# A sixth product term for head 3, a product buffer and counts for each of two sums, weights prepared on GpSimd, and other orders in the five engine loops

## The chip, the cores and the metric

The kernel runs on one core of a Trainium2 chip. The metric is the device time of one execution in microseconds (us), the median of a few executions. Work is issued to five engines that run their own instruction streams: TensorE (PE; its weight loads are shown as PEld), VectorE (DVE), ScalarE (ACT), GpSimd (POOL) and SyncE (SP, which only issues transfers). They wait for one another through semaphores.

## The reference, cut to what matters

Two sequences of 4096 tokens with 512 features go through a layer norm and then through two branches whose results are added to the input. All arithmetic is float32, H = 4 heads of 128.

```python
xn = layernorm(x)
# branch 1: attention by the delta rule in chunks of 32, with a convolution path
q, k, v = (silu(causal_conv4(xn @ W)) for W in (Wq, Wk, Wv))
delta_out = delta_rule_chunkwise(q, k, v, sigmoid(xn @ Wb))   # state S, triangular inverses
outs = [dwconv_causal(v, w) for w in (ms_w3, ms_w15, ms_w31)] # 3, 15 and 31 taps
ms_out = (per_head(concat(outs)) @ kernel_mix_w) @ channel_mixer_w
wts = softmax(gelu([xn, mean|ms|, mean|delta|, mean|v|] @ w1 + b1) @ w2 + b2)
o = rmsnorm(wts[0]*ms_out + wts[1]*delta_out + wts[2]*v) * o_norm_w
out = x + o @ Wo
# branch 2: token-shift FFN on xn
out += sigmoid(xr @ W_r) * (relu(xk @ W_k)**2 @ W_v)
```

## The kernel before, in words

The tokens are cut into 32 steps of 128 tokens of both sequences. Every engine runs the loop `for i in range(NS + 2)`, and three steps are in flight: in pass `i` the front of step `i` (norm, projections `project`, `copy_raw`), the middle of step `i - 1` and the end of step `i - 2`. There are 31 passes (i = 2 to 32) that hold all of middle and end. The order of the calls in each engine's loop is written out by hand, call by call, and it is the order in which the engine executes: an engine whose next instruction waits does nothing else.

**The tap sums.** The 3-, 15- and 31-tap convolutions make 12 blocks of 128 channels, three a head, in `my[h % 2]`. ScalarE writes the first tap (`first_taps`, L1106), VectorE adds the others one by one (`taps`, L1531, one instruction of 128x256 a tap). For some leading taps ScalarE makes the products instead (`multiply_taps`, L1117, three activations into `prod`), and GpSimd issues a DMA that adds `prod` to `my` (`add_taps`, L457). `LEAD[h]` says how many taps of a head VectorE does not do: one for heads 0 and 1, two for head 2 (one product), five for head 3 (four products). So there are five adding DMAs a step and 196 - 27 = 169 taps for VectorE. All products share one buffer `prod` and one count, so a product waits for the addition before it.

**The inverse.** ScalarE scales the Gram matrices (`scale_B`, L983). SyncE writes them to HBM and reads 64 blocks of 16 rows back (`rows_out`, `Bu`). GpSimd inverts the blocks column by column (`invert_units`, L431 to L439). SyncE writes and reads again (L355, then L364, four transfers into `Yq`). TensorE then joins blocks: `inverse_W` (L570), `inverse_Z` (L581), `join_W` (L590), `join_Z` (L602, L604), `half_W` (L613), `half_X` (L621), with small steps of VectorE (`turn_Y`, `mask_W`, `step_Y`) and ScalarE (`copy_W`, `spread_X`, `join_X`, `copy_half_W`, `join_half_X`) between them. `key_state` (L630) and `solve` (L637) need the full inverse.

**Other names of the argument.** `channel_mix` (L699) ends the convolution path; `copy_ms` reads it. `turn_o` (L746) transposes the normalized output (`normalize_o`, L1214, which needs GpSimd's `invert_o`); `attend` (L754) multiplies by Wo. `ffn_key` (L662) needs `mix_in` (L1507) from VectorE, which needs `mix_half` (L1072) from ScalarE. `project` (L516) runs in six pairs 0 to 5; pair 4 needs pair 2 copied (`copy_raw(i, 2)`, L894). `prepare_weights` (L1384 to L1395) runs once, on VectorE at the start of pass 2.

## Time and profile before

| | |
|---|---|
| time, median of 3 runs | 3527.82 us (3523.88 to 3529.14) |
| the profiled execution: its own time | 3519.07 us |
| its span, first to last instruction | 3517.3 us |
| mean granted TensorE clock | 0.98 |
| TensorE busy | 94% of the span |
| VectorE busy | 90% |
| ScalarE busy | 78% |
| GpSimd busy | 23% |

All times in the rows are counted from the start of the span. The busy share of an engine is a sum over stages; a step has about 105.5 us, and what ends the waits inside one step is read from the timeline of one step.

### The profile page before, as it was taken

To read this page: it belongs to the slowest core of one execution; us is meant where nothing else is said; L and a number is where in the kernel's file an instruction comes from. 1 tells how busy PE (TensorE), PEld (TensorE's weight loads), DVE (VectorE), ACT (ScalarE), POOL (GpSimd) and SP (SyncE) were. 2 spreads that over 40 slices of the span, in tenths; PEclk is the share of its full clock that TensorE was granted. 3 is DMA by queue.
4 is the path that set the end of the run, shared out by engine and by line. 5 is a ranking of instruction groups with operands and counts; after the bars stand their busy time and mean duration, and the time that the engine had idled before them with its cause. 6 is when DMAs were issued, how large, how long until landed. Compare 5 with 4: busy or idle time off the path is not lost.

```text
span 3517.3 us, 69963 instructions
## 1 busy us (share of the span) xinstructions
PE 3315.3 (94%) x22848; PEld 2447.8 (70%) x22848; DVE 3165.9 (90%) x7856; ACT 2758.2 (78%) x9144; POOL 807.7 (23%) x1489
## 2 busy tenths in 40 slices
PE   6899999999999999999999999999999999999986
PEld 5677777667777667776677776777766677767754
DVE  6999998999999999989999999999899899989993
ACT  5677888778887778787778887778877788877774
POOL 2022221122221222221222211222212222112220
PEclk8999999999999999999999999999999999999998
DMA  6022221122211122211222111222111222112220
GB/s 183 11 50 51 50 40 33 29 51 51 50 32 33 37 51 51 50 28 25 49 51 51 36 38 29 50 51 50 32 33 38 51 50 43 35 24 51 45 44 7
DMA packets 188307, 154.92 MB, mean 44 GB/s; under 512 B 111804, under 2 KB 146108, under 8 KB 187688
## 3 DMA queue, kind: packets, MB, share of 16 engines
q0 software_dynamic: 31744, 79.70, 13.1%
q1 hardware_dynamic: 156200, 70.76, 7.7%
q8 instruction: 182, 2.98, 0.3%
q14 instruction: 181, 1.48, 0.1%
HBM read 51.34 MB, written 52.95 MB: 30 GB/s over the span
## 4 chain that ended last, share of the span: by engine, by line
PE 35%; DVE 25%; ACT 21%; issue 9%; DMA 7%; POOL 2%; ACTq 0%; DVEq 0%; POOLq 0%; SPq 0%
DVE my L1531 19%; PE dense L721 6%; DMA my<-prod 5%; PE dense L674 5%; PE dense L678 5%; PE dense L662 3%; ACT my L1106 3%; PE small L690 2%; ACT dense L1136 2%; PE cell L644 2%; PE cell L645 2%; PE cell L637 2%; ACT kT L926 1%; DMA rows_out<-Bm 1%; ACT xsh L856 1%
## 5 line engine op out<-in xcount | busy, mean ns | idle before, releaser
L1531 DVE SCALAR_TENSOR_TENSOR my<-vT,mw,my 128x256 f32<-128x256 f32 x5408 | 2245.4, 480 | 38.9 <-DMA my<-prod 24.3
L721 PE MATMUL dense<-xsh,w 128*128 128x256 f32 x2048 | 483.2, 382 | 3.9
L397 POOL TENSOR_SCALAR vare<-xsq 128x2 f32<-128x2 f32 x32 | 6.2, 194 | 2081.8 <-ACT xsh L856 2081.8
L721 PEld LDWEIGHTS dense<-xsh,w 128*128 128x128 f32 x2048 | 369.4, 190 | 72.3 <-ACT xr L1168 11.1
L1079 ACT ACTIVATE ka<-dense 128x512 f32<-128x512 f32 x64 | 38.2, 597 | 319.3 <-PE dense L662 319.3
L662 PE MATMUL dense<-xk,wfk 128*128 128x256 f32 x1024 | 250.1, 400 | 22.0 <-DVE xb L1591 16.8
L662 PEld LDWEIGHTS dense<-xk,wfk 128*128 128x128 f32 x1024 | 198.4, 199 | 74.9 <-issue 47.0
L674 PE MATMUL dense<-wr,xr 128*128 128x512 f32 x512 | 235.4, 603 | 0.0
L516 PE MATMUL front<-xsh,wq 128*128 128x256 f32 x1024 | 231.9, 379 | 0.0
L678 PE MATMUL dense<-wfv,ka 128*128 128x512 f32 x512 | 230.2, 592 | 0.0
L516 PE MATMUL front<-xsh,wv 128*128 128x256 f32 x1024 | 228.7, 381 | 0.8 <-ACT xsh L871 0.8
L516 PE MATMUL front<-xsh,wk 128*128 128x256 f32 x1024 | 227.9, 379 | 1.4 <-ACT raw L894 1.4
L1117 ACT ACTIVATE prod<-vT,mw 128x256 f32<-128x256 f32 x480 | 211.0, 513 | 22.5 <-DMA my<-prod 22.0
L754 PE MATMUL dense<-wo,ms 128*128 128x512 f32 x512 | 228.2, 598 | 0.0
L699 PE MATMUL dense<-cm,ym 128*128 128x512 f32 x512 | 225.0, 592 | 0.0
L516 PEld LDWEIGHTS front<-xsh,wq 128*128 128x128 f32 x1024 | 192.0, 190 | 38.9 <-issue 14.8
L516 PEld LDWEIGHTS front<-xsh,wk 128*128 128x128 f32 x1024 | 193.5, 189 | 30.6 <-ACT raw L894 3.3
L516 PEld LDWEIGHTS front<-xsh,wv 128*128 128x128 f32 x1024 | 193.0, 191 | 27.3 <-issue 1.1
L457 POOL DMA_DIRECT2D my<-prod x160 | 146.4, 915 | 235.0 <-ACT my L1106 197.9
L690 PE MATMUL small<-my,km 128*128 128x256 f32 x768 | 193.0, 388 | 0.1
L439 POOL TENSOR_TENSOR Xu<-Xu,Tu 64x28 f32<-64x28 f32 (+3 forms) x448 | 182.4, 407 | 35.1
L436 POOL TENSOR_TENSOR Tu<-Bu,Xu 64x28 f32<-64x28 f32 (+3 forms) x448 | 181.7, 406 | 30.2
(182 smaller groups left out, 6803.2 us busy)
## 6 DMA issues: line engine op xcount, KB each, us to landing
my<-prod POOLq DMA_DIRECT2D x160, 384.0 KB, 4.2
xa<-in_x SPq DMA_DIRECT2D x32, 512.0 KB, 4.2
rows_out<-Bm SPq DMA_DIRECT2D x64, 256.0 KB, 4.3
out<-xb POOLq DMA_DIRECT2D x32, 512.0 KB, 14.7
Yq<-units_out SPq DMA_DIRECT2D x128, 32.0 KB, 2.1
w<-in_w SPq DMA_DIRECT2D x1, 2048.0 KB, 17.2
Bu<-rows_out SPq DMA_DIRECT2D x32, 64.0 KB, 2.9
units_out<-Xu SPq DMA_DIRECT2D x32, 64.0 KB, 2.5
```

The source lines that it names most:

```text
L436: e.tensor_tensor(Tu[:, 0:n, 0:j + 1], Bu[:, j, j + 1:HQ][:, :, None].broadcast_to([UNITS, n, j + 1]), Xu[:, j, 0:j + 1][:, None, :].broad ...
L439: left = e.tensor_tensor(Xu[:, j + 1:HQ, 0:j + 1], Xu[:, j + 1:HQ, 0:j + 1], Tu[:, 0:n, 0:j + 1], ALU.subtract)
L516: i = e.matmul(by_batch(front[pair % 2][:, c * W:(c + 1) * W]), wt[:, k, hs(c0 + c)], xsh[s % 2][:, k, :, 1:1 + P], start=(k == 0), stop=( ...
L662: i = e.matmul(dense[pair][:, c * W:(c + 1) * W], wfk[:, k, hs(2 * pair + c)], xk[:, k, :], start=(k == 0), stop=(k == CB - 1))
L674: i = e.matmul(dense[0][:, :], xr[:, k, hs(b)], wr[:, k, :], start=(k == 0), stop=(k == CB - 1))
L678: i = e.matmul(dense[1][:, :], ka[:, k, hs(b)], wfv[:, k, :], start=(k == 0), stop=(k == CB - 1))
L690: i = e.matmul(s_mix, km[:, p, :], my[h % 2][:, p, :], start=(p == 0), stop=(p == 2))
L699: i = e.matmul(dense[b][:, :], ym[:, k, hs(b)], cm[:, k, :], start=(k == 0), stop=(k == CB - 1))
L721: e.matmul(by_batch(o), w1[:, k, hs(2 * pair + c)], xsh[s % 2][:, k, :, 1:1 + P], start=(k == 0), stop=False)
L754: i = e.matmul(dense[b][:, :], ms[:, b, hs(h)], wo[:, h, :], start=(h == 0), stop=(h == H - 1))
L1117: i = e.activation(by_batch(prod[:, p, :]), vT[s % 2][:, c, :, off:off + P], ACT.Copy, scale=mw[:, col:col + 1])
L1531: i = e.scalar_tensor_tensor(o, vT[s % 2][:, c, :, off:off + P], mw[:, col:col + 1], o, ALU.mult, ALU.add)
```

## The change

`LEAD[3]` goes from 5 to 6: ScalarE makes one more product for head 3 (three activations), GpSimd issues one more adding DMA, VectorE does three taps less, in each step. Heads 0 and 2 on the one side, 1 and 3 on the other get a product buffer and a pair of counts of their own (`prod[h % 2]`, `tap_products[h % 2]`, `taps_added[h % 2]`). `prepare_weights` moves from VectorE to GpSimd, at the start of pass 2, and is written with other instructions (13 in place of 15 on the engine). The calls in the loops of GpSimd, TensorE, ScalarE and VectorE stand in another order.

```diff
-LEAD = (1, 1, 2, 5)
-ADDED = [sum(LEAD[:h]) - h for h in range(H + 1)]
+LEAD = (1, 1, 2, 6)
+ADDED = [LEAD[h] + LEAD[h + 2] - 2 for h in range(2)]
...
-        prod = sb("prod", P, 3, W)
+        prod = [sb(f"prod{i}", P, 3, W) for i in range(2)]
...
+        def add_index(h, r):
+
+            return r if h < 2 else LEAD[h - 2] - 1 + r
+
         def adds_before(s, h, r):
 
-            return taps_added, 16 * (s * ADDED[H] + ADDED[h] + r)
+            return taps_added[h % 2], 16 * (s * ADDED[h % 2] + add_index(h, r))
...
+            def prepare_weights():
...
+                e.wait_ge(split_in, 16 * (2 + PARTS * PARTS))
+                whole, taken = (t[0:NROW, :, :].rearrange("p b d -> p (b d)") for t in (ms, dl))
+                for k in range(CB):
+                    then(e.tensor_scalar(wo[:, k, :], wo[:, k, :], onw[:, 0:1], None, ALU.mult))
+                then(e.tensor_copy(ident16[:, :], ident))
+                then(e.tensor_copy(w1x[:, :], whole))
+                for j in range(1, PARTS):
+                    later = cst[0:NROW, C_PART + j:C_PART + j + 1]
+                    then(e.tensor_scalar(taken, w1x[:, :], later, None, ALU.mult))
+                    then(e.tensor_tensor(whole, whole, taken, ALU.subtract))
+                    then(e.tensor_copy(w1x[:, :], whole))
...
             def add_taps(s, h, r):
                 e.wait_ge(*tap_zero.upto(s, h))
-                e.wait_ge(*tap_products.upto(s, ADDED[h] + r))
-                e.dma_start(my[h % 2][:, :, :], prod[:, :, :], accum_op=ALU.add).then_inc(taps_added, 16)
+                e.wait_ge(*tap_products[h % 2].upto(s, add_index(h, r)))
+                e.dma_start(my[h % 2][:, :, :], prod[h % 2][:, :, :], accum_op=ALU.add).then_inc(taps_added[h % 2], 16)
...
+                if i == 2:
+                    prepare_weights()
...
             def multiply_taps(s, h, r):
 
-                if s or ADDED[h] or r:
+                if s or add_index(h, r):
                     e.wait_ge(*adds_before(s, h, r))
...
                 if c:
                     turn_o(i - 2, 0)
-                if f:
-                    project(i, 4)
-                if c:
                     turn_o(i - 2, 1)
                     attend(i - 2, 0)
                     attend(i - 2, 1)
```

**TensorE, from the last projections to the join.** Before, in the stretch from `project(i, 3)` on: `front<-xsh,wk` are the projections of pairs 2 and 3, `front<-xsh,wq` is `project(i, 4)`, `turn<-cst,vT` is `turn_tokens(i - 1, 3)`.

```order
L516 MATMUL front<-xsh,wk 128x256 x16
L746 MATMUL dense<-cst,dl 128x128 x4
L516 MATMUL front<-xsh,wq 128x256 x8
L746 MATMUL dense<-cst,dl 128x128 x4
L754 MATMUL dense<-wo,ms 128x512 x8
L662 MATMUL dense<-xk,wfk 128x256 x8
L570 MATMUL cell<-Yq,Bm 32x16 x32
L581 MATMUL cell<-Wq,Xq 32x16 x32
L662 MATMUL dense<-xk,wfk 128x256 x8
L590 MATMUL cell<-Yq,Bm 32x32 x16
L545 MATMUL turn<-cst,vT 128x128 x4
```

After (the same stretch; line numbers are those of the changed file, L786 is `attend`, L694 `ffn_key`, L602 and L613 `inverse_W` and `inverse_Z`, L622 `join_W`):

```order
L548 MATMUL front<-xsh,wk 128x256 x16
L662 MATMUL cell<-S,kT 128x128 x4
L778 MATMUL dense<-cst,dl 128x128 x8
L786 MATMUL dense<-wo,ms 128x512 x8
L577 MATMUL turn<-cst,vT 128x128 x4
L694 MATMUL dense<-xk,wfk 128x256 x8
L577 MATMUL turn<-cst,vT 128x128 x4
L602 MATMUL cell<-Yq,Bm 32x16 x32
L613 MATMUL cell<-Wq,Xq 32x16 x32
L622 MATMUL cell<-Yq,Bm 32x32 x16
```

`project(i, 4)` no longer stands between the two `turn_o`, `key_state(i - 1, 1)` stands ahead of them, both `turn_tokens` of v stand around the first `ffn_key`, and the second `ffn_key` no longer stands between `inverse_Z` and `join_W`.

**TensorE, from the join to the solve.** Before, from the last instruction of `join_Z`:

```order
L604 MATMUL cell<-Wq,Xq 32x32
L674 MATMUL dense<-wr,xr 128x512 x4
L678 MATMUL dense<-wfv,ka 128x512 x4
L613 MATMUL cell<-YW,Bm 64x64 x8
L621 MATMUL cell<-X,YW 64x64 x8
L630 MATMUL cell<-S,kT 128x128 x4
L637 MATMUL cell<-y,X 128x128 x8
```

After (L645 is `half_W`, L653 `half_X`, L706 and L710 `ffn_out(i - 1, 0)`, L662 `key_state(i - 1, 0)`):

```order
L636 MATMUL cell<-Wq,Xq 32x32
L694 MATMUL dense<-xk,wfk 128x256 x8
L645 MATMUL cell<-YW,Bm 64x64 x8
L548 MATMUL front<-xsh,wq 128x256 x8
L653 MATMUL cell<-X,YW 64x64 x8
L706 MATMUL dense<-wr,xr 128x512 x4
L710 MATMUL dense<-wfv,ka 128x512 x4
L662 MATMUL cell<-S,kT 128x128 x4
L669 MATMUL cell<-y,X 128x128 x8
```

The second `ffn_key` and `project(i, 4)` (L548) stand around `half_W` now, and `ffn_out` behind `half_X`.

**GpSimd, the second half of the inversion.** Before, from the eighth column's last subtraction (L457 is the adding DMA, `add_taps`):

```order
L439 TENSOR_TENSOR Xu<-Xu,Tu 64x6x10
L436 TENSOR_TENSOR Tu<-Bu,Xu 64x5x11
L439 TENSOR_TENSOR Xu<-Xu,Tu 64x5x11
L436 TENSOR_TENSOR Tu<-Bu,Xu 64x4x12
L439 TENSOR_TENSOR Xu<-Xu,Tu 64x4x12
L436 TENSOR_TENSOR Tu<-Bu,Xu 64x3x13
L439 TENSOR_TENSOR Xu<-Xu,Tu 64x3x13
L436 TENSOR_TENSOR Tu<-Bu,Xu 64x2x14
L439 TENSOR_TENSOR Xu<-Xu,Tu 64x2x14
L436 TENSOR_TENSOR Tu<-Bu,Xu 64x15
L439 TENSOR_TENSOR Xu<-Xu,Tu 64x15
L457 DMA my<-prod 128x768
```

After (L484 is the adding DMA):

```order
L463 TENSOR_TENSOR Tu<-Bu,Xu 64x5x11
L466 TENSOR_TENSOR Xu<-Xu,Tu 64x5x11
L484 DMA my<-prod 128x768
L463 TENSOR_TENSOR Tu<-Bu,Xu 64x4x12
L466 TENSOR_TENSOR Xu<-Xu,Tu 64x4x12
L463 TENSOR_TENSOR Tu<-Bu,Xu 64x3x13
L466 TENSOR_TENSOR Xu<-Xu,Tu 64x3x13
L463 TENSOR_TENSOR Tu<-Bu,Xu 64x2x14
L466 TENSOR_TENSOR Xu<-Xu,Tu 64x2x14
L463 TENSOR_TENSOR Tu<-Bu,Xu 64x15
L466 TENSOR_TENSOR Xu<-Xu,Tu 64x15
L484 DMA my<-prod 128x768
```

An adding DMA, that of head 3's fourth product, now stands inside the inversion; the fifth stands behind it, where the fourth stood.

## Rows read from the trace of the kernel before

**Rows 1.** Windows: stretch, its length, PE, PEld, DVE, ACT, POOL busy, granted clock.

```profile
1004.09:1109.57 105.48, 102.05 (x716) 75.34 (x715) 98.46 (x245) 86.10 (x286) 25.22 (x46) 1.00 0.21 42
1084.90:1109.57 24.67, 24.67 (x107) 16.08 (x106) 22.70 (x57) 20.62 (x76) 0.00 (x0) 1.00 0.00 1
```

**Rows 2.** Timeline of one step, VectorE: start, length, line, [idle before <-releaser].

```profile
1004.09 0.18 DVE L1541 TENSOR_TENSOR frest<-ft,fparts 128x24 f32<-128x24 f32 x1 [1.94 <-ACT fparts L1145]
...
1068.27 11.92 DVE L1531 SCALAR_TENSOR_TENSOR my<-vT,mw,my 128x256 f32<-128x256 f32 x30
```

**Rows 3.** Timeline of the same step, TensorE.

```profile
1048.00 0.66 PE L746 MATMUL dense<-cst,dl 128*128 128x128 f32 x4 [0.41 <-ACT dl L1214]
1048.49 3.63 PE L516 MATMUL front<-xsh,wq 128*128 128x256 f32 x16
1051.95 0.60 PE L746 MATMUL dense<-cst,dl 128*128 128x128 f32 x4
...
1059.98 3.69 PE L662 MATMUL dense<-xk,wfk 128*128 128x256 f32 x16 [0.55 <-DVE xb L1591]
1063.60 0.73 PE L570 MATMUL cell<-Yq,Bm 32*32 32x16 f32 x64
1064.82 0.72 PE L581 MATMUL cell<-Wq,Xq 32*32 32x16 f32 x64 [0.50 <-DVE Wq L1476]
1065.47 3.72 PE L662 MATMUL dense<-xk,wfk 128*128 128x256 f32 x16
1069.12 0.69 PE L590 MATMUL cell<-Yq,Bm 32*32 32x32 f32 x32
...
1079.90 1.14 PE L621 MATMUL cell<-X,YW 64*64 64x64 f32 x16 [0.68 <-ACT YW L1027]
1081.71 1.16 PE L630 MATMUL cell<-S,kT 128*128 128x128 f32 x8 [0.67 <-ACT X L1032]
```

**Rows 4.** Timeline of the same step, ScalarE.

```profile
1014.84 1.30 ACT L1117 ACTIVATE prod<-vT,mw 128x256 f32<-128x256 f32 x3
...
1021.32 0.84 ACT L1168 ACTIVATE xk<-dense,b 128x256 f32<-128x256 f32 x2 [0.97 <-PE dense L724]
...
1027.75 2.15 ACT L983 ACTIVATE Bm<-cell,g 128x128 f32<-128x128 f32 x8
...
1049.45 1.26 ACT L1214 ACTIVATE dl<-dl,rro 128x128 f32<-128x128 f32 x4
```

**Rows 5.** Timeline of the same step, GpSimd: the inversion's first and last, one adding DMA.

```profile
1037.29 0.44 POOL L431 TENSOR_SCALAR Xu<-Bu 64x15 f32<-64x15 f32 x1 [0.70 <-DMA Bu<-rows_out]
...
1050.23 0.93 POOL L457 DMA_DIRECT2D my<-prod  x1
...
1055.82 0.32 POOL L439 TENSOR_TENSOR Xu<-Xu,Tu 64x15 f32<-64x15 f32 x1
```

**Rows 6.** DMA view, stretch 1004 to 1110: issues, KB each, median us to landing.

```profile
my<-prod POOLq DMA_DIRECT2D x5, 384.0 KB, 4.3
...
Yq<-units_out SPq DMA_DIRECT2D x4, 32.0 KB, 2.2
```

**Rows 7.** Timeline of the same step, SyncE's queue.

```profile
1058.69 2.26 SPq L364 DMA_DIRECT2D Yq<-units_out  x4
```

**Rows 8.** Timeline at pass 2, VectorE (first and last of 15) and TensorE.

```profile
93.86 2.05 DVE L1384 TENSOR_SCALAR wo<-wo,onw 128x512 f32<-128x512 f32 x4
...
105.59 0.69 DVE L1395 CAST w1x<-dl 108x1024 bf16<-108x1024 f32 x1
...
106.66 1.06 PE L590 MATMUL cell<-Yq,Bm 32*32 32x32 f32 x32 [8.99 <-DVE Yq L1481]
```

**Rows 9.** Lines by form: two GpSimd instructions of different size, mean ns.

```profile
L439 POOL TENSOR_TENSOR Xu<-Xu,Tu 64x60 f32<-64x60 f32 x64 | 32.7, 511 | 5.0
L439 POOL TENSOR_TENSOR Xu<-Xu,Tu 64x15 f32<-64x15 f32 x32 | 10.3, 323 | 2.5
```

**Rows 10.** Windows, columns as in Rows 1: a stretch at the first join.

```profile
1489.40:1492.80 3.40, 3.40 (x10) 2.68 (x9) 3.36 (x10) 0.99 (x8) 0.00 (x0) 0.50 0.34 84
```

More of the change, by code:

```diff
@@ L777, in tensor_program @@
                 if c:
+                    hidden(i - 2, 1)
                     hidden(i - 2, 2)
@@ L820, in tensor_program @@
                 if k:
+                    turn_tokens(i - 1, 2)
                     ffn_key(i - 1, 0)
+                    turn_tokens(i - 1, 3)
                     inverse_W(i - 1)
                     inverse_Z(i - 1)
+                    join_W(i - 1)
+                    join_Z(i - 1)
                     ffn_key(i - 1, 1)
-                    join_W(i - 1)
-                    turn_tokens(i - 1, 3)
-                    join_Z(i - 1)
+                    half_W(i - 1)
+                if f:
+                    project(i, 4)
+                if k:
+                    half_X(i - 1)
                     ffn_out(i - 1, 0)
-                    half_W(i - 1)
-                    half_X(i - 1)
                     key_state(i - 1, 0)
@@ L1345, in scalar_program @@
                 if c:
+                    square_o(i - 2, 1)
+                    normalize_o(i - 2, 0)
                     normalize_o(i - 2, 1)
@@ new lines, in vector_program @@
+                    taps(i - 2, 3, 12, 14)
+                    taps(i - 2, 3, 15, 17)
+                    taps(i - 2, 3, 18, 20)
+                    taps(i - 2, 2, 36, 37)
+                    taps(i - 2, 3, 8, 9)
+                    taps(i - 2, 3, 21, 22)
+                    taps(i - 2, 2, 52, 53)
+                    taps(i - 2, 3, 22, 23)
+                    taps(i - 2, 3, 24, 25)
+                    taps(i - 2, 3, 11, 12)
+                    taps(i - 2, 3, 27, 28)
+                    taps(i - 2, 3, 14, 15)
@@ new lines, in vector_program @@
+                    taps(i - 2, 3, 25, 26)
+                    taps(i - 2, 3, 17, 18)
+                    taps(i - 2, 3, 28, 29)
+                    taps(i - 2, 3, 20, 21)
+                    taps(i - 2, 3, 30, 31)
+                    taps(i - 2, 2, 37, 38)
+                    taps(i - 2, 3, 31, 32)
+                    taps(i - 2, 3, 33, 34)
+                    taps(i - 2, 3, 23, 24)
+                    taps(i - 2, 3, 36, 37)
+                    taps(i - 2, 2, 53, 54)
+                    taps(i - 2, 3, 34, 35)
@@ L1691, in vector_program @@
                     taps(i - 1, 0, 0, 1)
+                    taps(i - 1, 1, 7, 8)
+                    taps(i - 1, 1, 6, 7)
                 if c:
@@ L1797, in vector_program @@
                 if k:
-                    taps(i - 1, 2, 36, 37)
-                    taps(i - 1, 2, 51, 52)
+                    mix_in(i - 1)
+                    taps(i - 1, 2, 47, 49)
                 if c:
@@ L1802, in vector_program @@
                 if k:
[L1803 to L1806 removed]
+                    taps(i - 1, 2, 30, 31)
+                    taps(i - 1, 2, 49, 50)
+                    taps(i - 1, 2, 34, 35)
+                    taps(i - 1, 2, 50, 52)
+                    taps(i - 1, 3, 1, 2)
+                    taps(i - 1, 3, 0, 1)
                     turn_Y(i - 1, 0)
                     mask_W(i - 1)
[L1809 to L1810 removed]
+                    taps(i - 1, 3, 4, 5)
+                    step_Y(i - 1)
+                    taps(i - 1, 3, 3, 4)
+                    turn_Y(i - 1, 1)
+                    taps(i - 1, 3, 7, 8)
         N_ZEROED = 13
[L1813 removed]
+        N_SCALED = CB + 2 + 3 * (PARTS - 1)
         plans = [tap_plan(h) for h in range(H)]
```

403 lines of the change are left out of this document (169 added, 234 removed).

## The prediction

> **What bounds the kernel now.** I read the table first: TensorE is busy for 94% of the span, VectorE for 90%. Such shares don't say which engine ends a step, so I took one step out of the middle, from one `frest` of VectorE, at 1004.09 [rows 2], to the next. It is 105.48 us long, and in it TensorE is busy 102.05 us, VectorE 98.46, ScalarE 86.10, GpSimd 25.22 [rows 1]. TensorE stands still for 3.4 us a step, all others for more. The last 24.67 us of the step have no gap on TensorE at all [rows 1].
>
> The second view is TensorE's timeline of that step [rows 3]. The reader is to look at the brackets: 0.41 us before `turn_o`, 0.55 before `ffn_key`, 0.50 between `inverse_W` and `inverse_Z`, 0.68 before `half_X`, 0.67 before `key_state`. From `inverse_W` at 1063.60 to the step's end only 1.85 us are gaps. So whatever is put into TensorE's queue behind `inverse_W` lengthens the step by its own length, except for what it fills of those 1.85 us.
>
> The third view says what `inverse_W` itself waits for. ScalarE ends `scale_B` at 1029.90 (1027.75 + 2.15) [rows 4]; the blocks go through HBM; GpSimd starts on them at 1037.29 and ends at 1056.14 (1055.82 + 0.32) [rows 5]; SyncE issues the four reads of `Yq` until 1060.95 (1058.69 + 2.26) [rows 7]; 2.2 us later they have landed [rows 6], at 1063.15. TensorE takes them at 1063.60. That leaves 0.45 us of slack. So a step has two parts in series: from the end of `channel_mix` over ScalarE, HBM, GpSimd and HBM to `Yq` (not shortened by an idle TensorE), and from `inverse_W` to the end of `channel_mix` (TensorE alone). The step is their sum.
>
> **The change, part by part.**
>
> *Three taps less on VectorE.* Thirty taps take 11.92 us [rows 2], 0.395 each from start to start, so 1.19 us a step go. VectorE is not on either part of the sum except in `turn_Y`, `mask_W` and `step_Y`; the relief is hidden under TensorE's work. Counted at 0; at most -1.19.
>
> *The sixth product.* Three activations take 1.30 us of ScalarE [rows 4], the issue of the DMA 0.93 us of GpSimd [rows 5], and it lands 4.3 us later [rows 6]. What counts is where it stands. Ahead of `scale_B`, the new order of ScalarE has one product and `first_taps(0)` more (2 x 1.3 us) and one `short_first` and some halo copies less (about 1.1 us, by my estimate from the 1.30 of three such activations); the wait of 0.97 us before `gelu_hidden` [rows 4], which was for TensorE, is filled by it. About 0.4 us more come from `copy_ms(1)` standing right behind `copy_ms(0)`. 2.6 - 1.1 - 0.97 - 0.4 is 0.1: `scale_B` ends where it did (-0.5 to +0.5). In GpSimd's stretch from `Bu` to the last column, three adding DMAs stand where two stood: +0.93. `Yq` lands at 1064.1, 0.45 us later than TensorE took it before. **+0.45** (0 to +1).
>
> *TensorE up to `inverse_W`.* `project(i, 4)` is gone from between the two `turn_o`. It took 3.46 us (1048.49 to 1051.95) [rows 3] there while ScalarE ended `normalize_o(1)`, at 1050.71 [rows 4]. Its new place in ScalarE's order brings it no earlier: `square_o(1)` waits behind a product that needs the previous addition, and GpSimd has an adding DMA between the two `invert_o`. I put its end at 1050.4. TensorE arrives at `turn_o(1)` at about 1048.2 and stands for 2.2 us. `attend` begins at 1051.0, `mix_in` still ends near 1059 since `mix_half` is behind the same work of ScalarE, `ffn_key(0)` ends at 1062.9, `turn_tokens` at 1063.3, and `Yq` is not there before 1064.1. Nothing is won in this part.
>
> *TensorE from `inverse_W` on.* Added: `project(i, 4)`, +3.46. Gone: `turn_tokens(3)`, four transposes like those of `turn_o`, 0.66 [rows 3]. Filled: the gaps of 0.68 and 0.67 in the half step, -1.35. The second `ffn_key` (3.65 us, 1065.47 to 1069.12 [rows 3]) no longer covers the hand-over from `inverse_Z` to `join_W`; `turn_tokens` no longer covers that to `join_Z`. The only such hand-over that is uncovered now, `mask_W`, costs 0.50 [rows 3]; the two others go the same way (one or two small VectorE instructions between two groups of small products), so 2 x 0.50 = +1.0 (+0.5 to +1.6). Together 3.46 - 0.66 - 1.35 + 1.0 = **+2.45**.
>
> A step becomes 2.9 us longer (range 1.5 to 3.9), 108.4 us. 31 passes: **+90 us** (47 to 121).
>
> *Weights on GpSimd.* On VectorE they took from 93.86 to 106.28, and TensorE stood for 8.99 us because `step_Y` was behind them [rows 8]. That stall goes: **-9**. GpSimd has 13 instructions over 9344 elements of a partition and can begin where VectorE did, near 93. `copy_o` of step 0 needs the result first. The join would now be near 98 (106.66 - 8.99), and behind it stand 10.8 us up to `half_X` and 1.8 more up to `key_state` in the old order (1069.12, 1079.90, 1081.71), with the 3.65 of `ffn_key` and the 3.46 of `project(i, 4)` added in the new one [rows 3]: about 118, and some 3 us of solve and outputs. No row has GpSimd at this size. Below, it needs the 12.4 us of VectorE; above, its slope between 15 and 60 elements, (511 - 323)/45 = 4.2 ns an element [rows 9], gives 39 us, which would end at 132 and cost some 11 us. I take it as hidden, because the slope comes from instructions that read through a stepped pattern, and plain rows should be nearer the low end. The Trainium skill, GPSIMD Engine Reference, section 3.1, has a two-input add of 2048 floats at 4497 ns on GpSimd and 2293 on VectorE; by that ratio the weights take about 25 us, end near 118, and stay hidden.
>
> The sum: own time 3519.07 + 90 - 9 = 3600. The runs' median stands 8.75 us above the profiled execution, so 3609.
>
> **The rivals.**
>
> *The relief reaches the end (faster).* For it: all of TensorE's 3.4 us a step are waits for others, VectorE is nearly as loaded as TensorE, and the half step's 1.35 us are filled in any case. It decides for it if `normalize_o(1)` ends 2 us earlier than I put it, so that no gap opens at `turn_o` and TensorE gets through its first part early, and if `Yq` is there by 1062, through an earlier `scale_B`. Then a step loses about 1.1 us: 3519 - 34 - 9 + 9 = 3485. Against it: the inversion's 18.85 us on GpSimd [rows 5] and four passages of HBM are the same. Chance 0.18.
>
> *Gains and losses cancel (no change).* `project(i, 4)` brings 3.46 us but lies where TensorE would stand anyway, because VectorE's taps for `kernel_mix` end the step. Against it: 24.67 us without a gap at the end [rows 1]. It needs +0.3 us a step: 3528. Chance 0.07.
>
> *The clock falls at the joins.* In a step further on, the granted clock was 0.50, its lower level (1.2 GHz), just after `inverse_W` [rows 10], and the `ffn_key` that stands there took 5.41 us in place of the 3.72 of [rows 3]. What came before were small products and a wait. In the new order four such groups with three waits follow one another, without `ffn_key`. If the clock falls once in most steps, that is +1.7 us each, 25 to 50 us: 3635 to 3660. In the half step the cause goes away, which pays part of it back. The Trainium skill, TensorE: Matmul & The Clock Gate, part 1, says that the array falls to half its clock when it has not been busy, which is the direction that the row shows. Chance 0.2, as a part of the slower case.
>
> *The five additions of head 3 come late.* Five rounds of 1.3 + 0.9 + 4.3 us [rows 4 to 6] are 32.5 us. The first product can be ready ahead of `first_taps(3)`, which stands behind `scale_B` and `normalize`, near 1031.6 in my count; so the fifth addition lands at 1063 to 1064. VectorE then stands for `taps(3)` in front of `turn_Y` for up to 1 us, at the very place where `Yq` arrives. It would add 0 to 31 us and is in the range.
>
> **How the numbers follow.** Slower by the sum above, with or without the clock: 0.75; faster 0.18; within 0.2% (7 us, about what a measurement of this kernel can tell) 0.07. The likeliest case's own range is 3560 (1.5 us a step) to 3660 (3.5 us a step and the clock). For eight times in ten I reach down to 3505.
>
> **What would show it.** Right: a step near 108.4 us; TensorE idle about 2 us before `turn_o`; gaps before `inverse_W`, `inverse_Z`, `join_W` and `join_Z`, together 2 to 3 us; none before `half_X` and `key_state`; VectorE idle more than the 7 us of a step now; no stall of 9 us at pass 2. Wrong: a step under 105 us, which would mean that `scale_B` ends earlier and moves `Yq` with it, or that TensorE's queue has less work behind `inverse_W` than I count.

## The result, and the profile after

The changed kernel takes 3692.39 us (median of 4 runs, 3689.91 to 3694.21), the kernel before 3525.9 in the runs beside it. The ratio is 1.0471, with a 95% interval from 1.0455 to 1.0486: slower by 166 us. I had forecast 3609 and a range up to 3660. The direction was right; the loss is twice what I worked out. Where a kernel had an execution in a slower state, at a lower clock, that one is left out of its median.

The profiled execution took 3689.91 us, with a span of 3688.1 and a mean granted clock of 0.955. The first view is the windows of the changed kernel, with the columns of [rows 1]: the prologue up to the first `frest`, the 31 steps, what is left, one step, and a stretch behind the joins of a later step.

```profile
0.00:153.60 153.60, 111.76 (x696) 86.83 (x697) 110.86 (x254) 85.79 (x266) 46.19 (x73) 0.88 0.41 113
153.60:3637.60 3484.00, 3247.69 (x22036) 2401.01 (x22034) 3026.80 (x7476) 2697.25 (x8909) 789.48 (x1455) 0.96 0.22 43
3637.60:3688.10 50.50, 27.69 (x118) 18.27 (x118) 6.86 (x16) 20.32 (x65) 3.63 (x5) 0.80 0.08 11
374.69:483.86 109.17, 103.59 (x716) 77.00 (x715) 98.10 (x242) 87.45 (x289) 25.20 (x47) 0.98 0.22 45
1111.00:1117.80 6.80, 5.01 (x68) 4.21 (x68) 6.80 (x19) 4.88 (x15) 0.00 (x0) 0.50 0.35 86
```

The kernel before has this row for its own 31 steps:

```profile
150.20:3465.50 3315.30, 3175.56 (x22036) 2344.31 (x22034) 3044.75 (x7570) 2653.12 (x8817) 778.88 (x1424) 0.99 0.21 41
```

Of the 170.8 us between the spans, the prologue holds +3.4, the steps +168.7, the rest -1.3. A step has 112.39 us on the mean (3484.00 / 31) against 106.94. TensorE is given the same 22036 matmuls and is busy 72 us longer with them, at a mean clock of 0.96 instead of 0.99. I added up the stretches at 0.50 in the record of the granted clock, by their place in a step, over the first 30 of the 31 steps (the last one has another 23.9 us before and 27.3 us after):

| kernel | behind `inverse_W` | near `turn_o` | half step | all |
|---|---|---|---|---|
| before | 6, 23.9 us | none | 10, 37.5 us | 61.4 us |
| changed | 29, 194.6 us | 13, 54.6 us | none | 249.2 us |

If TensorE had work in all of them, they cost half their length: 94 us of the 168.7 are the clock, 75 us (2.4 a step) are the rest. That is an estimate. A second way gives nearly the same: the 72 us of longer busy time, and 27 us more in which TensorE stands and waits for nothing that the profile shows. The changed kernel has 21 such places in its steps, the kernel before 7, and 17 of the 21 begin within 2 us of a fall of the clock. That this time goes with the clock is argued from the places alone. One ends at 1112.22, in the middle of the 32 products of `join_W`; it begins 0.1 us before a fall:

```profile
1112.22 0.53 PE L622 MATMUL cell<-Yq,Bm 32*32 32x32 f32 x12 [1.38 <-issue]
```

The second view is TensorE's timeline of the step at 374.69, one of the two shortest, with a single stretch of 3.4 us at 0.50; it answers to [rows 3].

```profile
418.67 0.60 PE L778 MATMUL dense<-cst,dl 128*128 128x128 f32 x4
420.87 0.66 PE L778 MATMUL dense<-cst,dl 128*128 128x128 f32 x4 [1.60 <-ACT dl L1243]
421.36 7.11 PE L786 MATMUL dense<-wo,ms 128*128 128x512 f32 x16
...
429.51 3.72 PE L694 MATMUL dense<-xk,wfk 128*128 128x256 f32 x16 [0.60 <-DVE xk L1511]
433.07 0.60 PE L577 MATMUL turn<-cst,vT 128*128 128x128 f32 x4
433.90 0.72 PE L602 MATMUL cell<-Yq,Bm 32*32 32x16 f32 x64 [0.23 <-DMA Yq<-units_out]
435.11 0.72 PE L613 MATMUL cell<-Wq,Xq 32*32 32x16 f32 x64 [0.50 <-DVE Wq L1480]
436.23 0.69 PE L622 MATMUL cell<-Yq,Bm 32*32 32x32 f32 x32 [0.40 <-DVE Yq L1485]
...
438.43 5.41 PE L694 MATMUL dense<-xk,wfk 128*128 128x256 f32 x16
443.77 1.14 PE L645 MATMUL cell<-YW,Bm 64*64 64x64 f32 x16
444.84 3.73 PE L548 MATMUL front<-xsh,wq 128*128 128x256 f32 x16
448.50 1.14 PE L653 MATMUL cell<-X,YW 64*64 64x64 f32 x16
```

Nearly each row is one that the prediction named. TensorE stands 1.60 us for `turn_o(1)`. `Yq` is the last to arrive at `inverse_W` (0.23). The four groups of small products follow with bare hand-overs. `project(4)` fills what was the gap in front of `half_X`. What I had only as a rival is the row at 438.43: the second `ffn_key` takes 5.41 us in place of 3.72. In most steps it is worse (5.94 on the mean of 29 steps; means over 29 steps leave out the first two of the 31).

### The profile page after: what moved, and what is told of

Same layout as the page of the kernel before. It is cut to its first block and busy times, and to the rows that moved or that the text cites. A ratio compares the mean times of both kernels' runs of the same rounds, so it can differ in the third digit from the quotient of the medians.

```text
span 3688.1 us, 70018 instructions
## 1 busy us (share of the span) xinstructions
PE 3387.1 (92%) x22848; PEld 2506.1 (68%) x22848; DVE 3144.5 (85%) x7745; ACT 2803.4 (76%) x9240; POOL 839.3 (23%) x1533
## 5 line engine op out<-in xcount | busy, mean ns | idle before, releaser
L694 PE MATMUL dense<-xk,wfk 128*128 128x256 f32 x1024 | 305.8, 463 | 23.2 <-DVE xk L1511 19.9
L1146 ACT ACTIVATE prod<-vT,mw 128x256 f32<-128x256 f32 x576 | 252.2, 506 | 81.2 <-DMA my<-prod 81.1
L694 PEld LDWEIGHTS dense<-xk,wfk 128*128 128x128 f32 x1024 | 236.4, 237 | 76.2 <-DVE xk L1511 19.1
L484 POOL DMA_DIRECT2D my<-prod x192 | 173.7, 905 | 373.8 <-ACT my L1135 291.4
L786 PE MATMUL dense<-wo,ms 128*128 128x512 f32 x512 | 250.5, 646 | 0.0
L548 PE MATMUL front<-xsh,wv 128*128 128x256 f32 x1024 | 231.9, 384 | 8.7 <-ACT xsh L900 8.6
L548 PE MATMUL front<-xsh,wq 128*128 128x256 f32 x1024 | 235.1, 382 | 0.0
L706 PE MATMUL dense<-wr,xr 128*128 128x512 f32 x512 | 233.6, 599 | 0.0
L548 PE MATMUL front<-xsh,wk 128*128 128x256 f32 x1024 | 230.4, 381 | 3.1 <-ACT raw L923 2.7
L710 PE MATMUL dense<-wfv,ka 128*128 128x512 f32 x512 | 230.2, 592 | 0.0
L548 PEld LDWEIGHTS front<-xsh,wv 128*128 128x128 f32 x1024 | 192.9, 191 | 41.2 <-ACT xsh L900 13.8
L548 PEld LDWEIGHTS front<-xsh,wq 128*128 128x128 f32 x1024 | 191.8, 190 | 40.9 <-issue 14.8
L548 PEld LDWEIGHTS front<-xsh,wk 128*128 128x128 f32 x1024 | 191.7, 190 | 36.6 <-ACT raw L923 10.8
L786 PEld LDWEIGHTS dense<-wo,ms 128*128 128x128 f32 x512 | 104.5, 210 | 123.5 <-issue 122.4
L1071 ACT ACTIVATE Bm<-cell,g 128x128 f32<-128x128 f32 x256 | 70.2, 369 | 154.0 <-PE cell L669 154.0
```

What stands on the lines that cost most here:

```text
L484: e.dma_start(my[h % 2][:, :, :], prod[h % 2][:, :, :], accum_op=ALU.add).then_inc(taps_added[h % 2], 16)
L548: i = e.matmul(by_batch(front[pair % 2][:, c * W:(c + 1) * W]), wt[:, k, hs(c0 + c)], xsh[s % 2][:, k, :, 1:1 + P], start=(k == 0), stop=( ...
L694: i = e.matmul(dense[pair][:, c * W:(c + 1) * W], wfk[:, k, hs(2 * pair + c)], xk[:, k, :], start=(k == 0), stop=(k == CB - 1))
L706: i = e.matmul(dense[0][:, :], xr[:, k, hs(b)], wr[:, k, :], start=(k == 0), stop=(k == CB - 1))
L710: i = e.matmul(dense[1][:, :], ka[:, k, hs(b)], wfv[:, k, :], start=(k == 0), stop=(k == CB - 1))
L786: i = e.matmul(dense[b][:, :], ms[:, b, hs(h)], wo[:, h, :], start=(h == 0), stop=(h == H - 1))
```

## The experiments

Seventeen kernels ran. "Changed" is the changed kernel; medians are compared with the runs of the kernel before beside them (3522 to 3529 us).

### The joins and the clock

**Bare joins alone.** The kernel before, with one piece of TensorE's new order. On ScalarE the two calls that take the result of `ffn_key(1)`, `relu_key(1)` and `square_key(1)`, move back with it, behind `copy_tokens(3)`:

```diff
                     inverse_Z(i - 1)
-                    ffn_key(i - 1, 1)
                     join_W(i - 1)
                     turn_tokens(i - 1, 3)
                     join_Z(i - 1)
+                    ffn_key(i - 1, 1)
```

> The kernel before with one part of the new order: ffn_key(1) behind join_Z instead of between inverse_Z and join_W (on ScalarE relu_key(1) and square_key(1) follow it, behind copy_tokens(3)); project(4), VectorE and GpSimd as before. The hand-over from inverse_Z to join_W is bare, +0.4 us a step, 12 us in all. Theory A (clock at the joins): in most steps a stretch at half clock is added there, which costs 1.7 to 3.4 us each beyond what the kernel before loses already, 3575 to 3635. Theory C (the clock is a by-product of lateness elsewhere in the changed kernel): 3530 to 3545.

Measured: 3632.25 us, ratio 1.0317 (1.0296 to 1.0337). TensorE's timeline of one of its steps:

```profile
1097.33 0.73 PE L570 MATMUL cell<-Yq,Bm 32*32 32x16 f32 x64
1098.55 0.72 PE L581 MATMUL cell<-Wq,Xq 32*32 32x16 f32 x64 [0.49 <-DVE Wq L1476]
1099.66 0.34 PE L590 MATMUL cell<-Yq,Bm 32*32 32x32 f32 x9 [0.40 <-DVE Yq L1481]
...
1103.22 5.62 PE L662 MATMUL dense<-xk,wfk 128*128 128x256 f32 x16
```

The stretches at 0.50 behind `inverse_W` go from 6 with 23.9 us to 30 with 211.6 us, the changed kernel's picture with nothing else of the change in it than the two calls on ScalarE. Over all steps 167 us more are at 0.50; half of them is 84 us, of the 108 by which the steps grew (again an estimate: TensorE is busy 62 us longer, and stands 16 us more for nothing that the profile shows). The rest are bare waits: 0.40 us a step in front of `join_W`, and 0.4 us in front of `turn_tokens(3)` for ScalarE. This is what the clock rival said, at about twice its price.

**Is it the idle time?** If waiting lets the clock fall, then something to do in the waits should hold it. Three products that nobody reads, first of 128 x 128, then of 128 x 256:

```diff
                     inverse_W(i - 1)
+                    busy(i - 1)
                     inverse_Z(i - 1)
+                    busy(i - 1)
                     join_W(i - 1)
+                    busy(i - 1)
                     turn_tokens(i - 1, 3)
```

> The kernel before with the bare joins (3632 us measured) and one extra product of 128 x 128 that nobody reads in each of the three waits of the joins. If idle time lets the clock fall, most of the 84 us of clock come back, 3550 to 3590; if small products alone are enough for it to fall, 3625 to 3645.

> The kernel before with the bare joins and one extra product of 128 x 256 in each of the same three waits as the run with 128 x 128. By itself the longer product costs up to 0.2 us a place beyond the wait, some 15 us. If full-size work in the joins holds the clock: 3570 to 3605. If it is only time that is added: 3635 to 3650.

Measured: 3623.7 us (the middle of 3618.08 to 3639.93) and 3618.84 us (3601.72 to 3624.14), against 3632.25 without; the gain of the small filler is not clear of the noise. The small filler leaves 208 us at 0.50 of the 229 in the first 30 steps, the long one 137, but that one adds its own length: 0.70 us a piece in the timeline, where the hand-overs have 0.4 to 0.6. So idle time alone isn't the cause; with hardly an idle stretch left between `inverse_W` and `join_W`, the clock still falls. The long filler holds it in part, and costs nearly what the clock gives back. The same filler in the changed kernel:

> The changed kernel with three extra products that nobody reads, one 128 x 256 product of 0.38 us ahead of inverse_Z, of join_W and of join_Z, each inside a hand-over of 0.40 to 0.58 us; no order is changed and no work is taken away. Theory A in the form that idle time in the joins lets the clock fall: the dips go, 3590 to 3620 us, and the hand-overs stay as long. If it is the small products that count as little work, whatever stands in the hand-overs: 3685 to 3705.

Measured: 3661.87 us (3640.89 to 3670.4), 249 us at 0.50 become 147. Half of that is 51 us; 31 are left over after what the fillers cost.

### Putting pieces of TensorE's order back into the changed kernel

**`ffn_key(1)` back between `inverse_Z` and `join_W`.**

```diff
-                    join_W(i - 1)
-                    join_Z(i - 1)
                     ffn_key(i - 1, 1)
+                    join_W(i - 1)
+                    join_Z(i - 1)
                     half_W(i - 1)
```

> The changed kernel with one call moved on TensorE: ffn_key(1) stands again between inverse_Z and join_W. Theory A, the clock at the joins: a full group of large products in the middle of the joins keeps the granted clock up; the hand-over of 0.40 us and the 2.2 us that ffn_key(1) loses at half clock go, together some 3 us a step, 3600 us (3585 to 3625). Theory B, the clock falls for another reason (the wait at turn_o, the small products themselves): only the hand-over comes back, 3670 to 3685. Theory C, the time is in what is late for TensorE, above all Yq: no change, 3692.

Measured: 3780.03 us, ratio 1.0722 (1.0688 to 1.0756): 88 us slower than changed, outside every theory of mine. TensorE's timeline shows the cause at once:

```profile
1146.77 0.22 PE L634 MATMUL cell<-Xq,Wq 32*32 32x32 f32 x2 [0.57 <-ACT Wq L1039]
1151.07 1.96 PE L645 MATMUL cell<-YW,Bm 64*64 64x64 f32 x16 [3.60 <-ACT YW L1050]
```

In the new order `ffn_key(1)` covers the 3.5 us that ScalarE needs between `join_Z` and `half_W` (`spread_X`, `join_X`), which in the kernel before the first `ffn_out` covered. Taken away, it leaves a wait of 3.60 us, after which `half_W` and part of `project(4)` run at half clock (1.91 us in place of 1.14 and 5.66 in place of 3.64, on the mean of 29 steps). I had looked at what the move lays bare, but not at what the changed kernel had put the piece there for.

**Both covers.** `project(4)` between `join_Z` and `half_W`, `ffn_key(1)` in the joins; on ScalarE `copy_raw(2)`, which takes a part of the projections, goes ahead of `copy_W`:

```diff
+                    ffn_key(i - 1, 1)
                     join_W(i - 1)
                     join_Z(i - 1)
-                    ffn_key(i - 1, 1)
-                    half_W(i - 1)
                 if f:
                     project(i, 4)
                 if k:
+                    half_W(i - 1)
                     half_X(i - 1)
```

> The changed kernel with ffn_key(1) between inverse_Z and join_W and project(4) between join_Z and half_W (copy_raw(2) on ScalarE moved ahead of copy_W, so that it isn't behind join_X). The 3.5 us from join_Z to half_W, which the run with ffn_key(1) alone laid bare, is covered by project(4); the gaps before half_X comes back (0.68). Against the changed kernel: -0.4 for a hand-over, +0.68, and under theory A about -2 us a step of clock: 3640 (3620 to 3665). If the clock falls for what comes before the inverse (the wait at turn_o): 3690 to 3710.

Measured: 3715.47 us. Now `half_X` waits, 2.09 us on the mean instead of the 0.68 of [rows 3], because in the new order ScalarE has `relu_key(0)` and `square_key(0)` ahead of `copy_half_W`. The stretches at 0.50 become 205 us, so by half their length 22 us of clock came back, and the wait took more.

**`project(4)` back between the two `turn_o`.** On ScalarE `copy_raw(2)` goes back ahead of `normalize_o`, too:

```diff
                     turn_o(i - 2, 0)
+                if f:
+                    project(i, 4)
+                if c:
                     turn_o(i - 2, 1)
...
                     half_W(i - 1)
-                if f:
-                    project(i, 4)
-                if k:
                     half_X(i - 1)
```

> The changed kernel with project(4) back between the two turn_o, and copy_raw(2) with its halo back ahead of normalize_o on ScalarE; the joins stay bare. My sum's term for project(4) was +3.46 behind inverse_W against 1.35 of filled gaps: without it a step loses 2.1 us, 3627 us. Theory A adds that the dips of the clock near the two turn_o go (about 12 of 31 steps, some 2 us each), 3600 to 3630. Theory C, Yq ends the first part of the step and project(4) would lengthen that part as much as it shortens the second: 3680 to 3700.

Measured: 3653.77 us (3633.33 to 3662.77), 38 us less than changed. All but two of the stretches near `turn_o` go, and the wait in front of `inverse_Z` grows: the new order leaves the fifth addition of head 3 late in 2 of 29 steps, by 9.35 and 9.65 us, and VectorE stands for it in front of `turn_Y`. That is my fourth rival; the changed kernel itself shows it only as short waits of VectorE, 0.1 to 1.5 us in 13 of its 31 steps, at the place where `Yq` arrives. The hand-over behind them stays at 0.50 us in every step, so they cost next to nothing. Then both moves together:

> Both moves of the two runs before it together: ffn_key(1) between inverse_Z and join_W, project(4) between the two turn_o. If the effects add and TensorE's order explains the loss, 3530 to 3550 us, within 1% of the kernel before. If VectorE's, ScalarE's and GpSimd's new orders hold a large part of it, over 3590.

Measured: 3771.56 us (3749.14 to 3793.55), ratio 1.0702 (1.0636 to 1.0767). The pieces don't add: the 3.5 us in front of `half_W` are bare here too, and 365 us of the steps are at 0.50.

`project(4)` back and the fillers of 128 x 256 in the joins, without the second move:

> The changed kernel with project(4) back between the two turn_o and the three extra products in the hand-overs of the joins: the two measured alone gave -38 and -30 us. If the bare joins cost clock by themselves, the effects add or more: 3600 to 3625. If both act on one cause, 3640 to 3655.

Measured: 3689.4 us, 36 more than with `project(4)` back alone. The late fifth addition comes in 5 steps, and `half_X` waits 1.24 us on the mean: TensorE reaches it sooner than ScalarE.

### The term for `project(4)`

The kernel before with one call moved:

```diff
                     turn_o(i - 2, 0)
-                if f:
-                    project(i, 4)
-                if c:
                     turn_o(i - 2, 1)
...
                     half_W(i - 1)
+                if f:
+                    project(i, 4)
+                if k:
                     half_X(i - 1)
```

> The kernel before with project(4) alone moved, from between the two turn_o to between half_W and half_X; nothing else on any engine. My sum: nothing won ahead of inverse_W because ScalarE and GpSimd set the end of turn_o(1) and Yq's arrival, and +3.46 - 0.68 = 2.8 us a step behind it, 3522 + 86 = 3608 (3590 to 3640 with some clock lost at turn_o). If TensorE gets through its first part earlier by what it no longer does there: 3522 to 3550.

Measured: 3595.43 us, ratio 1.0199 (1.0169 to 1.023). The timeline of a step near its middle:

```profile
1184.15 0.66 PE L746 MATMUL dense<-cst,dl 128*128 128x128 f32 x4 [1.95 <-ACT dl L1214]
1184.64 8.81 PE L754 MATMUL dense<-wo,ms 128*128 128x512 f32 x16
...
1212.39 3.73 PE L516 MATMUL front<-xsh,wq 128*128 128x256 f32 x16
1216.05 1.14 PE L621 MATMUL cell<-X,YW 64*64 64x64 f32 x16
```

The shortest step goes from 105.41 to 108.15 us: +2.74, where the sum says 3.46 - 0.68 = 2.78. What `project(4)` took at `turn_o` is waited out as predicted: in that step TensorE stands 2.20 us for `turn_o(1)` and 0.7 us more than before in front of the first `ffn_key`, and `inverse_W` begins where it did. In 22 steps the clock falls at `turn_o` (`attend` 8.81 instead of 7.03), though in the first 30 steps it no longer falls in the half step. This move alone costs 69 us and the bare joins alone 110; their sum, 179, is near the 166 of the whole change, which proves little, since the pieces didn't add when they were put back.

### VectorE and the sixth product

**The sixth product taken out of the changed kernel.**

```diff
-LEAD = (1, 1, 2, 6)
+LEAD = (1, 1, 2, 5)
...
-                    add_taps(i - 1, 3, 4)
...
-                    multiply_taps(i - 1, 3, 4)
...
-                    taps(i - 2, 3, 72, 75)
+                    taps(i - 2, 3, 72, 78)
```

> The changed kernel with the sixth product alone taken out (LEAD 5, four additions for head 3, the three taps back on VectorE at the end of its list); all orders else as changed. It prices the sixth product inside the new orders: my term was +0.45 us a step, so 3678 (3660 to 3690). If the product chain in front of normalize_o and turn_o is what TensorE waits for at 47 us of the step, as in the run with the sixth product in the old orders (4.9 us of wait there), 3600 to 3660. If VectorE needed the relief: 3700 to 3730.

Measured: 3712.87 us, ratio 1.0532 (1.0508 to 1.0555), 20 us more than changed. TensorE's timeline has one row in each step that the changed kernel hasn't:

```profile
1157.39 1.56 PE L721 MATMUL small<-my,km 128*128 128x256 f32 x6 [0.99 <-DVE my L1533]
```

The last `kernel_mix` waits for VectorE's taps. So in the new orders the sixth product, with the three taps that it takes off VectorE, is worth 20 us; I had counted the taps at nothing.

**The sixth product put into the kernel before**, two product buffers with it, products (3, 1) to (3, 4) one place earlier, their additions earlier on GpSimd, and VectorE's taps in an order that fits them:

```diff
-LEAD = (1, 1, 2, 5)
+LEAD = (1, 1, 2, 6)
...
                     copy_raw(i, 1)
+                if k:
+                    multiply_taps(i - 1, 3, 2)
                 if c:
                     square_o(i - 2, 0)
...
                     normalize_o(i - 2, 0)
                 if k:
-                    multiply_taps(i - 1, 3, 2)
+                    multiply_taps(i - 1, 3, 3)
```

> The kernel before with the sixth product alone: LEAD 6 for head 3, two product buffers and counts, three taps a step less on VectorE, the order of TensorE untouched; products and additions one place earlier on ScalarE and GpSimd to make room. My sum has +0.45 us a step for it (Yq later by one issue of 0.93 us on GpSimd), 3540 (3526 to 3556). If VectorE's relief reaches the end: 3500 to 3515. If the fifth addition is late for the taps in front of turn_Y: 3540 to 3580.

Measured: 3724.83 us, ratio 1.058 (1.0556 to 1.0605). ScalarE's and TensorE's timelines:

```profile
1103.39 1.31 ACT L1125 ACTIVATE prod<-vT,mw 128x256 f32<-128x256 f32 x3 [1.65 <-DMA my<-prod]
...
1107.66 1.28 ACT L1222 ACTIVATE dl<-dl,rro 128x128 f32<-128x128 f32 x4
1111.56 1.31 ACT L1125 ACTIVATE prod<-vT,mw 128x256 f32<-128x256 f32 x3 [2.62 <-DMA my<-prod]
```

```profile
1108.99 1.12 PE L754 MATMUL dense<-cst,dl 128*128 128x128 f32 x4 [3.46 <-ACT dl L1222]
```

Each product waits in ScalarE's queue for the addition before it, and `square_o` and `normalize_o` wait behind it. TensorE stands 4.88 us on the mean in front of `turn_o(0)` (3.48 in the middle one of the steps). How much of this is the product and how much my placing of it, this run doesn't separate. The new order has 2.3 us at the two `turn_o`, where the kernel before has 0.6 in most steps.

### The half step filled from other work

If only TensorE's length counts behind `inverse_W`, filling the gaps of 0.68 and 0.67 with work that is there anyway must give 42 us. In the kernel before, `ffn_out(0)` is cut up, and on ScalarE `copy_half_W` goes ahead of `scale_v` and `scale_v(0)` behind `join_half_X`:

```diff
-                    ffn_out(i - 1, 0)
+                    gate_out(i - 1)
+                    value_out(i - 1, 0, 2)
                     half_W(i - 1)
+                    value_out(i - 1, 2, 3)
                     half_X(i - 1)
+                    value_out(i - 1, 3, 4)
                     key_state(i - 1, 0)
```

> The kernel before with the half step filled in another way than by project(4): ffn_out(0) is cut into its gate products and two of four value products ahead of half_W, one between half_W and half_X, one between half_X and key_state; on ScalarE copy_half_W goes ahead of scale_v, and scale_v(0) behind join_half_X. The gaps of 0.68 and 0.67 go, the cover from join_Z to half_W shrinks from 7.2 to 5.4 us where ScalarE needs 5.2; nothing is added behind inverse_W. If what stands behind inverse_W counts by its own length, as my sum has it: 31 x 1.35 = 42 us less, 3480 (3470 to 3500). If scale_v or the shorter cover is late: 3515 to 3540.

> The run before it and one extra product of 0.38 us that nobody reads between inverse_W and inverse_Z, in a gap of 0.5 us. If idle time there is what lets the clock fall in the kernel before (24 stretches in its profile, about two thirds of them at this place), 10 to 30 us less than without it, 3455 to 3475; if not, the same time.

Then, on top of the first of these, a filling on TensorE, and in another kernel a shift on VectorE (`subtract_state(1)` goes up by one tap in the same way):

```diff
                     solve(i - 1, 1)
+                    kernel_mix(i - 1, 2)
                     solve(i - 1, 0)
```

```diff
                     taps(i - 2, 2, 54, 55)
+                    subtract_state(i - 2, 0)
+                    taps(i - 2, 3, 39, 40)
                     taps(i - 2, 3, 34, 35)
                     taps(i - 2, 3, 42, 43)
                     taps(i - 2, 3, 37, 38)
-                    subtract_state(i - 2, 0)
```

> The half step filled as in the run that cut ffn_out(0), and kernel_mix(2) moved from behind solve(0) to between solve(1) and solve(0), into the 1.34 us that TensorE waited there for scale_v(0) and subtract_state(0). If the step from inverse_W on is TensorE's own length, 1.2 to 1.3 us a step more are won: 3507 - 39 = 3468 (3460 to 3480). If the taps of head 2 that kernel_mix(2) needs end no earlier, VectorE takes the place: 3495 to 3507.

> The half step filled as in the run that cut ffn_out(0), and on VectorE subtract_state(1) one tap and subtract_state(0) four taps earlier in the list (the tap of head 2 that kernel_mix(2) needs stays ahead of it). If VectorE's list was what took the 1.34 us back: the wait in front of solve(0) goes, the shortest step falls from 105.4 to about 104.1, 3505 - 40 = 3465 (3460 to 3480). If the wait then shows up at another place again, or scale_v(0) on ScalarE is the one that is late: 3495 to 3507.

Measured:

| kernel | us | ratio, interval |
|---|---|---|
| half step filled | 3507.33 | 0.9947 (0.9925 to 0.9968) |
| and a filler at `inverse_Z` | 3503.21 | 0.9942 (0.992 to 0.9963) |
| half step filled, `kernel_mix(2)` between the solves | 3504.23 | 0.9936 (0.9914 to 0.9959) |
| half step filled, `subtract_state` earlier | 3521.95 | 0.9987 (0.997 to 1.0004) |

The gaps went as planned, yet the shortest of the first 30 steps stayed at 105.4 us (105.7 in the last version). The wait moved, first to the second `solve`:

```profile
1082.92 1.16 PE L637 MATMUL cell<-y,X 128*128 128x128 f32 x8 [1.34 <-DVE y L1504]
```

With `kernel_mix(2)` put in there, to `outputs`. VectorE's `y` ends at 1086.40, `solve(0)` begins at once, and `outputs` has to wait until ScalarE has copied its result, which `kernel_mix(2)` no longer covers (VectorE's timeline, then TensorE's):

```profile
1085.73 0.67 DVE L1504 TENSOR_TENSOR y<-y,cell 128x512 f32<-128x512 f32 x1
```

```profile
1086.45 1.16 PE L637 MATMUL cell<-y,X 128*128 128x128 f32 x8
1088.84 0.49 PE L644 MATMUL cell<-S,qT 128*128 128x128 f32 x2 [1.23 <-ACT Bm L1060]
```

With `subtract_state` earlier in VectorE's list, to the second `ffn_out` and the last `kernel_mix`, 1.25 us together:

```profile
1094.00 3.70 PE L674 MATMUL dense<-wr,xr 128*128 128x512 f32 x8 [0.56 <-DVE xb L1532]
...
1102.71 1.56 PE L705 MATMUL small<-my,km 128*128 128x256 f32 x6 [0.69 <-DVE my L1549]
```

Three fillings, and three times the same 1.3 us: at the next place where TensorE takes something from VectorE, or, in the second case, behind a `solve` that began when VectorE's part was there. From `turn_Y` to the last `kernel_mix` VectorE's list is as long as TensorE's; in the step of [rows 2] it has no gap there, and [rows 1] has VectorE busy for 22.70 of the last 24.67 us, with the 1.94 in front of `frest` [rows 2] as its only wait. The 20 us that were won are the clock: the stretches at 0.50 in the steps fell from 61.4 to 23.9 us, and none is left in the half step. The filler at `inverse_Z` changed nothing beyond that; its expectation put two thirds of the 24 stretches of the kernel before at the joins, and only 6 are there. The first three of the four versions beat the kernel before.

### The weights on GpSimd

The kernel before with `prepare_weights` alone moved:

```diff
             for i in range(NS + 2):
+                if i == 2:
+                    prepare_weights()
                 if f:
                     deviation(i)
```

> The kernel before with prepare_weights on GpSimd alone. The changed kernel's trace has it at 22.1 us there, ended at 115.7, before anything waited for it; my sum has -9 us for the stall of 8.99 us in front of join_W: 3517. If VectorE's taps are what the prologue waits for next, half of it or less comes through: 3520 to 3526. In the changed kernel the first frest came 3.4 us later than before, so something else there costs 12 us; here it is absent.

Measured: 3528.42 us, ratio 1.0007 (0.999 to 1.0025). The stall of 8.99 us [rows 8] is gone and a new one stands further on, in TensorE's timeline:

```profile
117.50 2.08 PE L661 MATMUL cell<-y,X 128*128 128x128 f32 x8 [4.15 <-DVE y L1485]
120.47 2.08 PE L661 MATMUL cell<-y,X 128*128 128x128 f32 x8 [0.90 <-DVE y L1485]
```

It waits for VectorE, whose 30 taps take 16.11 us there, not the 11.92 of [rows 2]. The first `frest` comes at 147.3 us in place of 150.2: of the 9 us some 3 are left, less than the medians can tell. In the changed kernel GpSimd's timeline and VectorE's timeline of the same stretch are these (the last two rows of VectorE are parts of the first, from narrower views):

```profile
93.52 6.81 POOL L412 TENSOR_SCALAR wo<-wo,onw 128x512 f32<-128x512 f32 x4
...
101.96 2.89 POOL L417 TENSOR_SCALAR dl<-w1x,cst 108x1024 f32<-108x1024 bf16 x1
104.93 2.65 POOL L418 TENSOR_TENSOR ms<-ms,dl 108x1024 f32<-108x1024 f32 x1
...
114.56 1.11 POOL L419 CAST w1x<-ms 108x1024 bf16<-108x1024 f32 x1
```

```profile
98.45 23.44 DVE L1535 SCALAR_TENSOR_TENSOR my<-vT,mw,my 128x256 f32<-128x256 f32 x37
103.32 0.87 DVE L1535 SCALAR_TENSOR_TENSOR my<-vT,mw,my 128x256 f32<-128x256 f32 x2
104.90 2.96 DVE L1535 SCALAR_TENSOR_TENSOR my<-vT,mw,my 128x256 f32<-128x256 f32 x2
```

Thirty-seven taps at 0.397 are 14.7 us; they took 23.44. Two taps that begin with the subtraction of 2.65 us on GpSimd need 2.96 us together, and the next one starts when it has ended. The multiplication at 101.96 holds VectorE up for its first half only: from 103.32 on, taps run beside it at their own pace, two in 0.87 us. So VectorE gives back 8.7 us while GpSimd does the work that VectorE was spared.

## Why the prediction was right, and where it was wrong

**What ends a step.** The chain over `Yq` and TensorE's queue behind `inverse_W` held: `Yq` ends a wait at `inverse_W` in 17 of the 18 steps of the changed kernel in which the clock doesn't fall at `turn_o`, and `project(4)` behind it came through at its own length (2.74 of 2.78 us). What failed is its reverse, that VectorE "is not on either part of the sum". Behind `inverse_W` the two engines' lists are equally long. A longer TensorE list lengthens the step, a shorter one doesn't shorten it, and relief on VectorE counts as soon as its list is the longer one (20 us in the changed kernel).

**`project(4)`, +3.46 - 1.35.** Right, shown by moving it alone. So, in the main, was the stand at `turn_o`: 2.2 us forecast for `turn_o(1)`, and 2.3 on the mean of 29 steps for the two together, 1.6 of it at `turn_o(1)`. What was left out is the clock that falls there when `project(4)` no longer stands between them (13 steps in the changed kernel, 22 in the run with the move alone).

**Hand-overs, 2 x 0.50.** They are 0.40 and 0.58. All four gaps of the joins are 1.7 us together, a little under the 2 to 3 that I had given as a sign.

**Up to `inverse_W`, +0.45.** It begins 60.86 us after `frest` on the mean, against 59.81: +1.05. In the 18 steps without a fall at `turn_o` it begins at 60.34, +0.5 as forecast. In the 13 others it begins at 61.62, behind an `attend` of 8.65 us in place of 7.18: there TensorE is late and hardly waits for `Yq`.

**The sum of the steps.** I had +2.9 a step; without the clock the changed kernel has +2.4 by the estimate above. This part of the forecast (90 us) stands at 75. (The range of 1.5 to 3.9 isn't the sum of the ranges of its terms, which is 1.95 to 4.05, or down to 0.76 with the taps; the measured value is inside all of them.)

**The clock at the joins, the step that failed.** It stood as a rival with 0.2, at "once in most steps, +1.7 us each, 25 to 50 us", and only as an upper addition. The runs show one in 29 of 30 steps, of 3.4 to 10.2 us, and a second kind at `turn_o`: some 94 us more than before, by half the length of the stretches. I took one length of 3.4 us from [rows 10] as the price, without a reason that a stretch should end so soon. Of the 29 behind `inverse_W` 23 are at least twice as long. The direction could be had from the trace of before, and a chance of 0.2 was too low for it. The Trainium skill, TensorE: Matmul & The Clock Gate, part 1, has the clock fall by how busy the array has been; the fillers agree in so far as the short one did little and the long one more.

**The weights on GpSimd, -9.** The time on GpSimd was right (93.52 to 115.67 is 22.15 us, inside 12.4 to 39, near the 25 that I had estimated with the Trainium skill, GPSIMD Engine Reference, section 3.1), though the instructions are 12 and not 13, and the slope behind the 39 was no slope: in the view of [rows 9] 64 elements take 380 ns, less than the 511 of 60. "Hidden" was wrong: I asked what waits for GpSimd and not what GpSimd holds up. The first `frest` came at 153.6 instead of 150.2. Against the forecast that is 12.4 us too late. The taps' slowing can explain up to 8.7 of it (TensorE stands 2.76 and 2.21 us for `y` behind it), and 3.5 stand further ahead, where the first `ffn_key` begins at 89.12 instead of 85.60; which of the new orders does that isn't settled.

**The fifth addition late, 0 to 31 us.** It shows as short waits in the changed kernel, and costs next to nothing there. To cost 9 us in a step it needs a TensorE order that differs (2, 2 and 5 steps in three of the runs).

**Open.** What in the small products lets the clock fall, if not the idle time alone. How the sixth product's cost in front of `turn_o` divides between the product and its place.

## What to carry to other kernels

Before moving a call out of a chain of small products, write down what it covers at both ends: a full-size product between small ones pays for the hand-over and for TensorE's clock behind it, and the second was the dearer (some 84 of 108 us). Don't price a fall of the clock by the length of one stretch: here they lasted from 3.4 to 10.2 us. When two engines' lists end together, as 94% and 90% busy can mean, work added to TensorE cost its full length here and gaps filled on it gave nothing; a wait that goes to the next meeting point unchanged in size is the sign. And work moved to GpSimd isn't free for VectorE: price the taps that run beside it.

## What the runs showed of the hardware

A VectorE operation with two SBUF inputs, which takes 0.40 us from start to start, waited out a whole GpSimd instruction where that was a subtraction with two inputs: 2.96 us for two of them beside a subtraction of 2.65. Beside a cast of 1.11 us one of them took 1.25. Beside a multiplication by a scalar of 2.89 us it waited only for the first half. Together, 37 of them took 23.44 us in place of 14.7. The Trainium skill, SBUF — State Buffer, section "SBUF: two separate sides", calls the pair of ports that the two share an exclusive lock held for the instruction; the trace agrees for the subtraction and the cast, and not for the multiplication, beside whose second half taps ran at their own pace.

Three groups of 32-row products with waits of 0.4 to 0.6 us between them were enough to bring the granted clock from 1.0 to 0.50 (1.2 GHz) in nearly every step, and products of 128 x 128 in the waits didn't stop it: 208 us at the lower level instead of 229. Close to many of the falls TensorE also stood for up to 3.5 us for nothing that the profile shows (32 us in the steps of the changed kernel, 6 in those of the kernel before).
